# A selective scan on one Trainium2 core: two of eight input products made with diagonals on TensorE, and its PSUM banks shared in another way

## The reference

```python
def step(h, inp):
    x_t, dt_t, B_t, C_t = inp
    dA = jnp.exp(dt_t[..., None] * A)
    dBx = dt_t[..., None] * B_t[:, None, :] * x_t[..., None]
    h = dA * h + dBx
    y = jnp.einsum('bdn,bn->bd', h, C_t)
    return (h, y)
...
y = (ys + D_param[None, :, None] * xc) * jax.nn.silu(z)
return jnp.einsum('bdl,hd->blh', y, out_proj_w)
```

## Time and profile before

| | us |
|---|---|
| median of 3 runs | 5355.45 |
| lowest and highest | 5345.69, 5359.83 |
| the profiled execution | 5354.56 |
| its span, first to last instruction | 5352.8 |

### The profile page before, as it was taken

One profiled execution on the slowest core, in us unless ns is written; L12 is line 12 of the kernel. 1 busy time (PEld: TensorE's weight loads), 2 busy tenths in 40 slices (PEclk: granted clock), 3 DMA queues, 4 the chain that ended last, 5 costly groups with the idle time before them and its releaser, 6 DMA issues. The chain is left out here.

```text
span 5352.8 us, 40461 instructions
## 1 busy us (share of the span) xinstructions
PE 4902.7 (92%) x14496; PEld 2349.2 (44%) x14496; DVE 3251.4 (61%) x3534; ACT 1881.3 (35%) x2677; POOL 2309.7 (43%) x1219
## 2 busy tenths in 40 slices
PE   8998989999868899968789999999999999999998
PEld 4443234467536444423333444444444344457443
DVE  1663468756457322239999999999999722103522
ACT  1554620045322111125555555555555410002100
POOL 1003420000022000019999999999999742100421
PEclk8899999999989999989999999999999999999999
DMA  2001030000010121142116436444644320000001
GB/s 75 1 1 67 32 118 24 28 17 1 9 34 1 40 68 67 50 123 53 42 40 174 133 124 179 140 133 134 181 140 124 127 82 0 24 0 27 22 16 47
DMA packets 180006, 360.84 MB, mean 67 GB/s; under 512 B 21790, under 2 KB 56734, under 8 KB 175710
## 3 DMA queue, kind: packets, MB, share of 16 engines
q1 hardware_dynamic: 171742, 330.45, 20.4%
q0 software_dynamic: 8064, 27.80, 1.4%
HBM read 300.50 MB, written 57.67 MB: 67 GB/s over the span
## 5 line engine op out<-in xcount | busy, mean ns | idle before, releaser
L2851 POOL TENSOR_TENSOR l2scan_h<-l2scan_dtx,l2scan_Bb 128x1024 f32<-128x1024 f32 x512 | 1198.2, 2358 | 30.8 <-DMA l2scan_Bb<-l_bc 15.0
L2753 PE MATMUL l2scan_yp<-l2scan_h,ident 128*128 128x512 f32 x2048 | 971.5, 608 | 115.1 <-POOL l2scan_h L2876 101.1
L2820 ACT ACTIVATE l2scan_ring<-l2scan_dt,l2scan_A 128x512 f32<-128x512 f32 x1024 | 663.9, 681 | 639.4 <-DVE l2scan_h L2932 481.0
L2753 PEld LDWEIGHTS l2scan_yp<-l2scan_h,ident 128*128 128x128 f32 x2048 | 389.3, 193 | 639.4 <-issue 481.1
L2743 PE MATMUL l2scan_low_z<-state,l2scan_Wz 128*128 128x512 f32 x1024 | 476.6, 598 | 0.3
L2876 POOL TENSOR_TENSOR l2scan_h<-l2scan_h,l2scan_Cb 128x1024 f32<-128x1024 f32 x192 | 452.1, 2355 | 8.6 <-DVE l2scan_h L2921 0.9
L2411 PE MATMUL l2in_acc<-state,l2in_W 128*128 128x512 f32 x1024 | 444.9, 595 | 10.5 <-DMA l2in_W<-l_attn_in_x 10.5
L2932 DVE TENSOR_TENSOR l2scan_h<-l2scan_ring,l2scan_Cb 128x1024 f32<-128x1024 f32 (+1 forms) x384 | 394.3, 1041 | 6.1 <-DMA l2scan_Cb<-l_bc 0.7
L2921 DVE TENSOR_TENSOR_SCAN l2scan_ring<-l2scan_ring,l2scan_carry,l2scan_h 128x512 f32<-128x512 f32 x320 | 392.7, 1273 | 0.0
L2921 DVE TENSOR_TENSOR_SCAN l2scan_ring<-l2scan_ring,l2scan_h 128x512 f32<-128x512 f32 x320 | 373.3, 1212 | 5.5 <-POOL l2scan_h L2851 5.5
L2538 PE MATMUL l2scan_oacc<-l2scan_oy,l2scan_oW 128*128 128x512 f32 x768 | 353.1, 592 | 0.0
(11 more groups left out here) (409 smaller groups left out, 7538.2 us busy)
## 6 DMA issues: line engine op xcount, KB each, us to landing
l2scan_oy<-l_y SPq DMA_DIRECT2D x192, 512.0 KB, 4.9
l2scan_Wz<-l_attn_in_z SPq DMA_DIRECT2D x64, 512.0 KB, 3.6
l2scan_oW<-l_attn_out_w SPq DMA_DIRECT2D x192, 128.0 KB, 3.3
l_xc<-l2in_xc SPq DMA_DIRECT2D x16, 1024.0 KB, 4.8
l2scan_xc<-l_xc SPq DMA_DIRECT2D x64, 256.0 KB, 5.7
l2scan_Bb<-l_bc SPq DMA_DIRECT2D x128, 128.0 KB, 6.9
l2scan_Cb<-l_bc SPq DMA_DIRECT2D x128, 128.0 KB, 7.8
l_y<-l2scan_zs SPq DMA_DIRECT2D x64, 256.0 KB, 5.5
```

The lines of the kernel that those rows point to most:

```text
L2753: last = t.matmul(yp[:, :], K.ident[:, :], h[:, st % SLOTS, j, :], start=g == 0 and j == 0, stop=g == NSG - 1 and j == SGR - 1)
L2820: a.activation(bank(st, j), dt[:, q % 2, :], ACT.Exp, scale=A[:, ct, n:n + 1]).then_inc(dA_ok, 1)
L2851: g_.tensor_tensor(h[:, st % SLOTS], dtx[:, None, :].to_broadcast([P, SGR, NT]), Bb[:, g * SGR:(g + 1) * SGR, :], ALU.mult).then_inc(dBx_o ...
```

## The change

Pair 7 becomes a W pair (GpSimd multiplies by C instead of VectorE). A second string, `MAKERS`, says who makes dBx: for P as before, for T (pairs 3 and 7) TensorE. For that TensorE transposes dtx in four blocks (`turn_dtx`), ScalarE copies it to SBUF (`keep_dtx`), and `spread` multiplies each block with a diagonal matrix of B values into the ring's bank; ScalarE's exponential goes into the slot of h instead. ScalarE makes the 16 diagonals once per chunk (`diagonals`) from a transposed piece of the low-rank tensor (`turn_rows`, `columns`). The sums over states are taken by 64 passes of 128 columns in transpose mode that accumulate in `yT`; ScalarE copies them (`keep`) and TensorE turns them back (`turn_back`). The bank `small` serves dt, softplus, both turns and the turned sums by turns, `big` serves z and the out projection. z is computed early in even items and late in odd ones, and the out projection in six parts between. `finish` moves from g = 1 to g = 6, `add` from g = 6 to g = 4. SyncE's order follows.

The diff, cut to its core:

```diff
-KINDS = "YWYWYWYY"
+KINDS = "YWYWYWYW"
+MAKERS = "PPPTPPPT"
...
-    HELD = 2
+    SHARE = (1, 1, 2, 1, 2, 1)
...
-        yp = s.ps("yp", [P, NT])
-        low_z = s.ps("low_z", [P, NT])
-        oacc = s.ps("oacc", [P, NT])
+        yT = s.ps("yT", [P, BLOCKS, P])
+        small = s.ps("small", [P, NT])
+        big = s.ps("big", [P, NT])
...
@@ SyncE, in the loop over items @@
+                    if q % 2 == 0 and q >= CT:
+                        late = range(at + 5, at + PIECES)
+                        for n in range(at, at + 3):
+                            proj.load(e, n)
+                    if q % 2 == 0 and q + 2 < ITEMS:
+                        z_weights(q + 2)
+                    if q % 2 == 0 and q >= CT:
+                        for n in range(at + 3, at + 5):
+                            proj.load(e, n)
...
+                    if q:
+                        store(q - 1)
+                    if q + 2 < ITEMS:
+                        channels(q + 2)
+                        dt_weights(q + 2)
...
+                    for n in late:
+                        proj.load(e, n)
...
+                    if q % 2 and q + 2 < ITEMS:
                         z_weights(q + 2)
...
@@ TensorE @@
                 def dt_tile(q):
-                    if q >= 2:
-                        t.wait_ge(z_ok, q - 1)
-                    elif q:
-                        t.wait_ge(dt_ok, q)
+                    if q:
+                        t.wait_ge(dx_ok, q)
...
                 def z_part(q, k0, k1):
                     if k0 == 0:
                         t.wait_ge(wz_in[q % 2], 16 * (q // 2 + 1))
-                        t.wait_ge(dt_ok, min(q + 2, ITEMS))
-                        if q == ITEMS - 1:
+                        if q:
                             t.wait_ge(z_ok, q)
+                        if q % 2 and q >= CT:
+                            t.wait_ge(proj.added, (q - CT) // 2 + 1)
...
+                def out_part(q, i):
+                    tile = (q - CT) // 2
+                    if i == 0:
+                        t.wait_ge(z_ok, q + 1)
+                    for n in proj.pieces(tile, i):
+                        proj.matmuls(t, n)
...
                 def total(st):
                     wait_hC(t, st)
                     if g == 0 and q:
-                        t.wait_ge(y_ok, q)
-                    for j in range(SGR):
-                        last = t.matmul(yp[:, :], K.ident[:, :], h[:, st % SLOTS, j, :], start=g == 0 and j == 0, stop=g == NSG - 1 and j == SGR - 1)
+                        t.wait_ge(copied, q)
+                    for j in range(SGR):
+                        for k in range(BLOCKS):
+                            last = t.matmul(yT[:, k, :], h[:, st % SLOTS, j, k * P:(k + 1) * P], K.ident[:, :], is_transpose=True,
+                                            start=g == 0 and j == 0 and k == 0, stop=g == NSG - 1 and j == SGR - 1 and k == BLOCKS - 1)
+                    last.then_inc(summed, 1)
...
+                def turn_dtx(q):
+                    t.wait_ge(dtx_ok, q + 1)
+                    if q % CT == 0:
+                        t.wait_ge(bt_ok, q // CT + 1)
+                    t.wait_ge(dt_ok, q + 1)
+                    if q >= 2:
+                        t.wait_ge(y_ok, q - 1)
+                    for k in range(BLOCKS):
+                        last = t.transpose(small[:, k * P:(k + 1) * P], dtx[:, k * P:(k + 1) * P], K.ident[:, :])
+                    last.then_inc(dx_ready, 1)
+
+                def spread(st):
+                    q, g = divmod(st, NSG)
+                    t.wait_ge(dg_ok, q // CT + 1)
+                    t.wait_ge(dx_ok, q + 1)
+                    for j in range(SGR):
+                        i = SGR * MAKERS[:g].count("T") + j
+                        wait_bank(t, st, j)
+                        for k in range(BLOCKS):
+                            last = t.matmul(bank(st, j)[:, k * P:(k + 1) * P], dtxT[:, k, :], dg[:, i, k, :], start=True, stop=True)
+                    last.then_inc(dBxT_ok, 1)
+
+                def turn_back(q):
+                    t.wait_ge(copied, q + 1)
+                    t.wait_ge(dt_ok, min(q + 3, ITEMS))
+                    t.wait_ge(dx_ok, min(q + 2, ITEMS))
+                    if q:
                         t.wait_ge(y_ok, q)
+                    for k in range(BLOCKS):
+                        last = t.transpose(small[:, k * P:(k + 1) * P], ysb[:, k, :], K.ident[:, :])
+                    last.then_inc(turned_back, 1)
...
@@ TensorE, in the loop over steps @@
+                    s16 = g + NSG * (q % 2)
+                    if g == 5 and q:
+                        turn_back(q - 1)
                     if g != 1 and st >= 2:
                         total(st - 2)
                     if g == 0 and st:
                         total(st - 1)
+                    if st + 1 < STEPS and maker(st + 1) == "T":
+                        spread(st + 1)
                     if g == 1 and q + 1 < ITEMS:
                         dt_tile(q + 1)
+                    if g == 7 and q + 1 < ITEMS:
+                        turn_dtx(q + 1)
+                    if s16 in (1, 13):
                         z_part(q, 0, 3)
+                    if s16 in (2, 14):
                         z_part(q, 3, 6)
+                    if s16 in (3, 15):
                         z_part(q, 6, KT)
+                    if 5 <= s16 < 11 and q >= CT:
+                        out_part(q - q % 2, s16 - 5)
...
@@ ScalarE @@
+                def keep(q):
+                    a.wait_ge(summed, (q + 1) * NSG)
+                    if q:
+                        a.wait_ge(turned_back, q)
+                    a.activation(ysb[:, :, :], yT[:, :, :], ACT.Copy).then_inc(copied, 1)
+                def keep_dtx(q):
+                    a.wait_ge(dx_ready, q + 1)
+                    if q:
+                        a.wait_ge(dBxT_ok, made("T", q * NSG - 1))
+                    a.activation(dtxT[:, :, :], small[:, :].rearrange("p (k d) -> p k d", d=P), ACT.Copy).then_inc(dx_ok, 1)
...
+                            for k in range(BLOCKS):
+                                last = a.activation(dg[:, i, k, :], K.ident[:, :], ACT.Copy, scale=BT[:, k, n:n + 1])
...
@@ ScalarE, in the loop, after the step's two exponentials @@
-                    if g == 1 and q:
-                        gate(q - 1)
-                    if g == 3 and q + 1 < ITEMS:
-                        split(q + 1)
+                    if g == 0 and q and ct == 0:
+                        columns(c)
+                    if g == 2:
+                        if q:
+                            keep_dtx(q)
+                        if q and ct == 0:
+                            diagonals(c)
+                        if q and q % 2 == 0:
+                            gate(q - 1)
+                    if g == 3:
+                        if q:
+                            keep(q - 1)
+                        if q + 1 < ITEMS:
+                            split(q + 1)
                     if g == 4 and q + 1 < ITEMS:
                         log1p(q + 1)
+                    if g == 6 and q % 2 == 0:
+                        gate(q)
...
@@ VectorE @@
+                        dA, dBx = (bank(st, j), hs[:, j, :]) if maker(st) == "P" else (hs[:, j, :], bank(st, j))
+                        last = v.tensor_tensor_scan(out, dA, dBx, init, ALU.mult, ALU.add)
...
-                    if g == 1 and q:
+                    if g == 6 and q:
                         finish(q - 1)
...
-                    if g == 6 and q >= CT and q % 2 == 1:
+                    if g == 4 and q >= CT and q % 2 == 1:
                         proj.add(v, (q - CT) // 2)
```

More of the change, by code:

```diff
@@ L2539, in matmuls, with pieces @@
         last.then_inc(self.used, 1)
-    def before(self, q):
-        return (q - CT) * PIECES // 2 - (self.HELD if q % CT == 1 else 0)
+    def pieces(self, tile, i):
+        at = tile * PIECES + sum(self.SHARE[:i])
+        return range(at, at + self.SHARE[i])
     def add(self, v, tile):
@@ L2695, in _ @@
                     c, ct = divmod(q, CT)
-                    ahead = range(proj.before(q + 1), proj.before(q + 2)) if CT <= q + 1 < ITEMS else ()
-                    if q:
-                        store(q - 1)
-                    if q + 2 < ITEMS:
-                        channels(q + 2)
-                    if ct == 1 and c and c + 1 < CHUNKS:
-                        low_rank(c + 1)
-                    if q + 2 < ITEMS:
-                        dt_weights(q + 2)
-                    for n in ahead[:proj.RING]:
-                        proj.load(e, n)
+                    at = (q - CT) // 2 * PIECES
+                    late = ()
+                    if q % 2 == 0 and q >= CT:
[7 more added lines that the diff above has]
+                            proj.load(e, n)
                     if ct == CT - 1 and c + 1 < CHUNKS:
@@ L2805, in gate, with columns, diagonals @@
                         a.wait_ge(y_out[q % 2], 16 * (q // 2))
```

(24 more changed lines are left out.)

95 lines of the change are left out of this document (62 added, 33 removed).

## The result

| | before | after |
|---|---|---|
| median of 4 runs each, us | 5356.30 | 5516.24 |
| the profiled execution | 5354.56 | 5513.62 |
| its span | 5352.8 | 5511.8 |

The ratio after to before is 1.030, 95% interval 1.0278 to 1.0322: the change makes the kernel slower by 3.0%. Forecast were 5455 us (5320 to 5560) and slower with 0.75. Direction and range held; the added time was 160 us and not 100.

What follows compares the result with a forecast made beforehand. VectorE, TensorE and GpSimd were taken as full together in the scan, with waits at pair 3 replacing the saved work. 65 + 12 − 13 + 13 + 3 + 2 + 18 = +100 us on 5354.56 gave 5455, range 5320 to 5560.

Steps and rivals of the forecast that it cites:

- The even item's wait: VectorE at pair 3 in even items waits 3.3 us for TensorE's spread(3), behind z and the sum of pair 0.
- I am wrong if spread(7) is waited for as well: Sign against the forecast: VectorE also waiting at pair 7 for TensorE's diagonal product, forecast to end at 26.95, wanted at 27.56.
- The odd item, "VectorE waits 4.2 us": Pair 3 of odd items, chunks 1 to 3: spread(3) drained at 13.86 us, VectorE waits 4.2, the item takes 31.42.
- The walk: Step-by-step timing of one item through the engines' queues, from VectorE's start on pair 0: mean 30.68 us against 28.66.
- Chunk 2, "+12": Chunk 2, without carries: items of 29.4 and 31.0 us, mean 30.2 against 29.46, +12 us.
- chunk 0, "−13": Chunk 0: odd items don't wait at pair 3 and take GpSimd's 26.9 us; mean 28.15 against 28.98, −13 us.
- Spread(7) just fits: Pair 7: TensorE's product ends at 26.95 us, VectorE wants it at 27.56; only a lower clock makes waits, about 0.5 to 0.8.
- The first item, "taken 3": Very start of the scan: diagonals and turns stand ahead of the first exponential; between 0 and 7 us, taken 3.
- Chunk starts, "16 x 0.275 = 4.4": Starts of chunks 1 to 3: 16 diagonal copies on ScalarE, 4.4 us, ahead of gate, z and spread(3); +13 us.
- SP's queue: nothing: SyncE's queue: z weights and five pieces go ahead of store, channels and dt weights; costed at nothing, else up to 2 us per even item.
- B (faster): Rival, chance 0.14: the chain to spread(3) is short enough, VectorE's 26.9 us per item decides; −100 us, 5255.
- C: Rival, chance 0.09: TensorE's clock falls during short transposes and waits, 3 us more in each of 64 items, 5647; doubled wholly, 5845.

Runs made afterwards that it cites:

- The first edit: The changed kernel with `spread(3)` issued on TensorE at g = 1, right behind dt: 5434.8 us, ratio 1.0143 to the kernel before.
- the best kernel: Changed kernel with spread(3), pair 0's sum, gate, diagonals, z's first weights, dt's weights and GpSimd's addition of dt all earlier: 5288.5 us, ratio 0.9865.

## Why the prediction was right, and where 60 us came from

**The mechanism** was right, and so was the reason for it: engines with less work per item, and a wait at pair 3 in the place of the work saved. VectorE's busy time fell by 1.3 us per item as forecast and GpSimd's by 2.1 (2.3); TensorE's fell by 0.8 and not 2.3, with the granted clock at 0.95 in chunks 1 and 2. Prices held: eight transposes 3012.13 − 3011.23 = 0.90 beside 0.87; sixteen instructions of `spread` 1.79 from start to start; T scans 2.45 for two like the others, so swapped inputs cost nothing; the copies 0.57 and 0.58. The even item's wait was 3.3 us forecast, 3.26 to 3.33 measured in chunks 1 and 3. ScalarE's copy of dtx started 0.63 us after the exponential ahead of it (0.6).

Two of its signs came out the other way. "I am wrong if spread(7) is waited for as well": it was, in 31 of 64 items. And in chunk 0 VectorE waited at pair 3 in the odd items too.

**By chunk**, from first scan to first scan. Chunk 1: 3383.03 − 2867.96 = 515.1 us against 458.5, so +57 (forecast 32 for waits, 4.4 for diagonals, 4 of the clock: 41). Chunk 2: 3895.47 − 3383.03 = 512.4 against 471.4, +41 (20). Chunk 3 to the end of the stage: +52 (43). Up to chunk 1's start: 2867.96 − 2858.40 = +10 (−4); as the scan began 8 us earlier in this execution, chunk 0 itself cost 18. Together 159, or 167 in the scan, forecast 100.

**The steps that were mis-sized**, each a term of the sum:

*The odd item, "VectorE waits 4.2 us".* It waited 4.27 to 5.72 us in chunk 1, 4.72 to 9.15 in chunk 2 and 4.56 to 5.28 in chunk 3: 27 us more than forecast over 24 odd items. The walk costed three pieces of the out projection and no data for them. Ahead of chunk 1's third wait stands (TensorE; the first row is that order, the second the wait that it ends in):

```profile
3040.04 3.70 PE L2536 MATMUL l2scan_big<-l2scan_oy,l2scan_oW 128*128 128x512 f32 x8 [1.13 <-DMA l2scan_oy<-l_y]
```

```profile
3046.44 2.45 DVE L3064 TENSOR_TENSOR_SCAN l2scan_h<-l2scan_h,l2scan_carry,l2scan_ring 128x512 f32<-128x512 f32 x2 [5.72 <-PE l2scan_ring L2817]
```

Up to the product of dt every link of this item is within 0.1 us of the walk; the wait for the piece is what the walk lacks. TensorE waited for such a piece in 17 of the 24 odd items, 0.34 to 1.13 us each, 11.8 in all. That the piece's DMA is late fits the three buffers that it has, but no run gave it more, so that cause is argued and not shown. The longest wait, 9.15 us in chunk 2, had dt's weights 1.60 us late and then two pieces at 5.40 us instead of 3.70. The rest is some tenths at each hand-over.

*Chunk 2, "+12", and chunk 0, "−13".* Chunk 2 exceeds its forecast by 21 us through terms listed here: the odd items' waits (14), `spread(7)` (5) and its start (3). In chunk 0 the odd item was to be set by GpSimd's 26.9 us, with `spread(3)` drained at 9.0 and no wait. Two items took 2529.45 − 2470.43 = 59.02 us, 29.5 each; the step had 28.15. In odd items `spread(3)` was waited for by 0.8 to 2.3 us, 10.1 in eight of them. TensorE stood waiting for GpSimd's product with C of pair 7, which this change gave it, and then ran the dt product at the lower clock (TensorE, an odd item that waited 1.00 us; the two dt instructions take 1.71 from start to start, 0.86 in the earlier trace rows):

```profile
2550.14 1.69 PE L2784 MATMUL l2scan_yT<-ident,l2scan_h 128*128 128x128 f32 x8 [3.27 <-POOL l2scan_h L3015]
2551.62 1.92 PE L2755 MATMUL l2scan_small<-l2scan_ssm,l2scan_Wdt 128*128 128x512 f32 x2
```

*"Spread(7) just fits".* It fitted in even items only. In odd ones VectorE waited 0.2 to 1.9 us in chunks 1 to 3 and 0.9 to 2.7 in chunk 0, 26 and 13 us in all, where 12 and 6 were forecast. TensorE's order of time (odd item of chunk 1):

```profile
2990.29 0.63 PE L2827 MATMUL l2scan_small<-ident,l2scan_ysb 128*128 128x128 f32 x4 [3.94 <-issue]
2990.75 1.86 PE L2784 MATMUL l2scan_yT<-ident,l2scan_h 128*128 128x128 f32 x8
2992.40 3.64 PE L2766 MATMUL l2scan_big<-state,l2scan_Wz 128*128 128x512 f32 x6
```

The 4 us of idle time before `turn_back` were forecast, and the lower clock behind them: eight transposes take 1.65 instead of 0.87, z's six have 3.64 instead of 2.74. Its size was taken at less than half.

*The first item, "taken 3".* That term was for the diagonals ahead of the first exponential: the first scan started 11.2 us after VectorE's first instruction of the scan before, 15.8 after, so 4.6. The larger part stood in no term: the load of z's weights, 14.5 us by the run that moved it. z was followed through TensorE, and its weights' place on SyncE's queue was not looked at for this item.

*Chunk starts, "16 x 0.275 = 4.4".* The diagonals took 4.77, and z then started 5.30 us late at the lower clock, which the step left out:

```profile
2872.80 4.77 ACT L2923 ACTIVATE l2scan_dg<-ident,l2scan_BT 128x128 f32<-128x128 f32 x16
```

```profile
2879.62 5.46 PE L2766 MATMUL l2scan_big<-state,l2scan_Wz 128*128 128x512 f32 x6 [5.30 <-ACT l2scan_zs L2898]
```

VectorE's waits there were 10.16, 10.52 and 8.41 us, some 7, 7 and 5 above the ordinary even item's: 19 and not 13.

*"SP's queue: nothing"* held at the chunk starts, for another reason than given. In the last item of a chunk the weights of dt stand behind the rows' waits, and TensorE did wait for them (3.9 and 4.4 us at two starts); the diagonals hid it. Inside the chunks the term was not nothing: the late pieces and the one late load of dt's weights are in the odd items' waits above, and the first item's 14.5 us are the place of a load on this queue.

Together these come to some 80 us, less about 8 that the forecast had for GpSimd in chunk 0 and that didn't come: near the 67 missing in the scan.

**The rivals.** B (faster) needed the wait at pair 3 below 1.5 us; that came about only with the order changed, and then at 5349 and not at its 5255, since other waits of about 1 us fill in. C fell. Its chance stood on a rule that no row had shown.

## What to carry to other kernels

Less work on every full engine is worth nothing while one instruction with a short need stands at the end of a long queue: the sixteen instructions of `spread`, moved ahead of z (or two pieces of the out projection) and one sum, gave back 81 us, and one GpSimd addition of 1.3 us, moved ahead of a product, 42. Where banks are shared by turns, write down for each turn who must have finished, and put the operation that the next engine wants first on its queue, not in the order of its step's number. And when a wait is taken away, look at what the same chain holds next. The first edit took away 258 us of waits for `spread` and gave 81; GpSimd's addition took away 56 and gave 42; dt's weights, moved alone, gave none, and pair 7's product ahead of z took away 17 us of waits and cost 15.

## What the runs showed of the hardware

240 fp32 transposes of 128 columns in a row kept the granted clock at 1.00 and 0.109 us each. An fp32 product against a diagonal of 128 columns costs 0.112. TensorE ran at the lower level again behind idle times of 3.94 us (eight transposes 1.65 us instead of 0.87, z's six instructions 3.64 instead of 2.74) and of 5.30 us (z's six 5.46). By these two rows an idle time behind a shared bank costs about one and a half times its length, an estimate. In the best kernel the granted clock of chunk 0 (2382 to 2858 us) is 0.83, lower than 0.93 before, and that chunk is still some 4 us shorter than before.
